# Five units of the first attention group scored between the qkv tiles, the attention output turned in the values' banks, and the second inverse root by Newton steps on VectorE

## What is computed

```python
x = x + attn(cond(x, cond_1024))             # cond: gated experts; attn: 16 heads of 16
x = x + ffn(cond2(x, cond_1024[:, None, :])) # cond2: a scan over the sequence; ffn: top-1 of 8 experts

# attn
qkv = x @ w_qkv.T                            # (B, N, 3, H, D), D = 16
q, k = rms_norm(q), rms_norm(k)              # t * rsqrt(mean(t * t) + eps)
attn = softmax((q @ k.T) * D ** -0.5)
y = attn @ v
Vn = v / max(norm(v), 1e-12)
y = y - sum(y * Vn) * Vn
out = y @ w_proj.T
```

## Time and profile before

| | |
|---|---|
| timed runs | 841.95, 844.62, 845.19 us |
| profiled execution, its own time | 842.52 us |
| its span in the trace | 840.8 us |
| TensorE busy | 779.9 us (93%) |
| ScalarE busy | 525.8 us (63%) |
| VectorE busy | 460.7 us (55%) |
| GpSimd busy | 248.3 us (30%) |
| first to last exponential of the attention | 329.12 to 582.80 us |

### The profile page before, as it was taken

The page is one execution under the profiler, slowest core; times in us unless marked ns, Lnnn a source line. Parts: engine busy times, 40 slices in busy tenths (PEclk is TensorE's granted clock), DMA queues, the critical chain, the costliest instruction groups (busy, mean ns, idle before and its releaser), DMA issues.

```text
span 840.8 us, 13450 instructions
## 1 busy us (share of the span) xinstructions
PE 779.9 (93%) x4456; PEld 511.6 (61%) x4456; DVE 460.7 (55%) x828; ACT 525.8 (63%) x699; POOL 248.3 (30%) x308
## 2 busy tenths in 40 slices
PE   8999999998999999889999989998789799999995
PEld 5778888886777875233222222223645588888884
DVE  3887666478766651533201202202447589999994
ACT  4432222463223236988999999997435288888883
POOL 5344444233433404200000000000000347777762
PEclk9999999999999999999999999999999899999999
DMA  9041111100234038064551342300178931111000
GB/s 251 18 77 51 50 49 43 34 26 26 101 113 135 4 43 107 1 115 162 76 76 27 49 75 36 39 0 0 51 266 283 337 126 49 52 51 53 25 11 0
DMA packets 52674, 64.87 MB, mean 77 GB/s; under 512 B 15889, under 2 KB 43929, under 8 KB 52636
## 3 DMA queue, kind: packets, MB, share of 16 engines
q1 hardware_dynamic: 44564, 55.96, 26.5%
q0 software_dynamic: 3312, 6.31, 2.5%
q10 hardware_dynamic: 4760, 2.12, 0.9%
HBM read 51.52 MB, written 15.60 MB: 80 GB/s over the span
## 4 chain that ended last, share of the span: by engine, by line
PE 67%; ACT 13%; DVE 9%; issue 8%; DMA 2%; ACTq 0%; SPq 0%; POOLq 0%; DVEq 0%
PE psum L1575 45%; ACT pexp L874 10%; PE psum L1727 7%; PE psum L1715 4%; PE psum L1931 2%; PE psum L1831 2%; DVE hl L1023 2%; DVE hh L1172 1%; PE psum L1845 1%; PE psum L1781 1%; DVE yT L1271 1%; PE psum L1678 1%; DMA x_tm<-in_x 1%; DVE ssum L1212 1%; DMA xs<-x_d,token_s 1%
## 5 line engine op out<-in xcount | busy, mean ns | idle before, releaser
L874 ACT ACTIVATE pexp<-psum 128x1024 f32<-128x1024 f32 x256 | 237.7, 1090 | 12.9 <-PE psum L1715 12.8
L801 ACT ACTIVATE hid<-psum,b_col 128x512 f32<-128x512 f32 x96 | 66.0, 688 | 160.5 <-PE psum L1575 107.2
L1727 PE MATMUL psum<-pexp,v_ones 128*32 128x512 f32 x1024 | 137.2, 609 | 18.5 <-ACT pexp L874 11.5
L1172 DVE TENSOR_SCALAR hh<-hid,scale_col 128x341 fp32r<-128x341 f32 x192 | 69.4, 403 | 70.5 <-ACT hid L801 53.6
L1715 PEld LDWEIGHTS psum<-q_stack,k_stack 48*128 48x128 f32 x512 | 39.2, 185 | 110.4 <-ACT pexp L874 92.8
L1715 PE MATMUL psum<-q_stack,k_stack 48*128 48x512 f32 x512 | 95.7, 449 | 7.2 <-DVE parts L1265 3.5
L1023 DVE SCALAR_TENSOR_TENSOR hl<-hid,scale_col,hh 128x341 fp32r<-128x341 f32 x192 | 96.3, 543 | 3.4
L1575 PE MATMUL psum<-hh,w2h 128*128 128x512 f32 x192 | 76.4, 398 | 4.0 <-DVE hl L1023 3.9
L1575 PE MATMUL psum<-x_hi,w1h 128*128 128x512 f32 x192 | 77.5, 404 | 0.1
L1575 PE MATMUL psum<-x_hi,w1l 128*128 128x512 f32 x192 | 75.6, 394 | 0.0
L1575 PE MATMUL psum<-x_lo,w1h 128*128 128x512 f32 x192 | 75.4, 393 | 0.0
(11 more groups left out here) (277 smaller groups left out, 1478.3 us busy)
## 6 DMA issues: line engine op xcount, KB each, us to landing
w_all<-in_L_ffn_W SPq DMA_DIRECT2D x16, 1024.0 KB, 12.9
raw<-in_L_cond_ew SPq DMA_DIRECT2D x32, 256.0 KB, 3.1
parts_d<-parts SPq DMA_DIRECT2D x8, 1024.0 KB, 5.0
q_stack<-parts_d SPq DMA_DIRECT2D x48, 128.0 KB, 4.7
k_stack<-parts_d SPq DMA_DIRECT2D x48, 128.0 KB, 7.4
raw<-in_L_cond_sw SPq DMA_DIRECT2D x16, 256.0 KB, 3.5
x_d<-x_tm SPq DMA_DIRECT2D x2, 1024.0 KB, 5.0
x_d<-x_tm ACTq DMA_DIRECT2D x4, 512.0 KB, 3.6
```

What stands on the lines that cost most here:

```text
L801: act.activation(hid[k % 4][:], bank(k % 4), ACT.Gelu_apprx_tanh, bias=b1_col[:, bass.ds(4 * q + k // 2, 1)]).then_inc(gelu_done, 1)
L874: act.activation(pexp[mt % 2][:, 2 * j:2 * j + 2, 512 * h:512 * h + 512], psum[:, 2 * r:2 * r + 2, :], ACT.Exp, scale=D ** -0.5)\
L1172: ins = dve.tensor_scalar(hh[k % 4][:, x0:x1], hid[k % 4][:, x0:x1], w[r], None, ALU.mult)
L1727: ins = pe.matmul(psum[VW * j:VW * j + VW, 6 + h, :], v_ones[i][:, mt, j, :], pexp[mt % 2][:, j, 512 * h:512 * h + 512], start=(mt == 0), ...
```

## The change

1. Scores of units 0 and 1 of group 0 are made behind qkv tile 4, unit 2 behind tile 5, unit 3 behind tile 6 and unit 4 behind tile 7 (`EARLY`), in banks 0 and 1 or 6 and 7; their exponentials stand between ScalarE's copies. The exponential of `decay` stands behind the copies of tile 0.
2. The ring starts with unit 5 and runs on over all groups. The output's turn goes to banks 6 and 7 behind unit 5 of the next group and takes no slot. Turns of q and k stand behind units 14 and 22 of groups 1 and 2. Blocks of values have a table: in groups 1 to 7 block 0 stands behind unit 8, and the next behind 9, 11, 12, 14, 15, 16, 18 and so on by twos; blocks 14 and 15 behind units 0 and 2 of the next group.
3. For batch 1, `root(1)` and the reciprocal are replaced by `inverse_root`: an integer first guess and three Newton steps, 14 instructions on VectorE over 256 elements per partition.
4. The groups are written out on TensorE and ScalarE instead of a loop; GpSimd's preparation of `v_ones` no longer waits for the qkv copies; SyncE's stores of the parts move to its steps for groups 2 and 3; the two matmuls of L1749 go.

```diff
+UNITS = HG * LT
+QK_AT = [(1, 14), (1, 22), (2, 14), (2, 22)]
+VALUES_AFTER = [8, 9, 11, 12, 14, 15] + [2 * v + 4 for v in range(6, LT + LT)]
+FIRST_VALUES_AFTER = [6, 7] + [2 * v + 4 for v in range(2, LT + LT)]
+EARLY = {4: (0, 1), 5: (2,), 6: (3,), 7: (4,)}
+EARLY_PAIR = (0, 3, 0, 3, 0)
+TURN_AFTER = 5
...
+        def pair(entry):
+            n = order.index(entry)
+            return EARLY_PAIR[n] if n < len(EARLY_PAIR) else (n - len(EARLY_PAIR) + 1) % 3
...
             sp.wait_ge(unit_done, 2 * FC * STEPS)
             for g in range(GROUPS):
                 load_stacks(g)
-                if g == 1:
-                    store_parts(1, 0)
-                if g == 2:
-                    for k in range(1, 4):
-                        store_parts(1, k)
+                if 2 <= g <= 3:
+                    for k in range(2):
+                        store_parts(1, 2 * g - 4 + k)
...
-            pool.wait_ge(qkv_out, TT)
+            pool.wait_ge(unit_done, 2 * FC * STEPS)
...
                 if g == 1:
+                    pool.wait_ge(qkv_out, TT)
...
+            def exp_unit(g, u):
+                mt, h, j = u // HG, u % HG // 2, u % 2
+                r = pair(("scores", g, u))
+                act.wait_ge(scored, UNITS * g + u + 1)
+                if u % 2 == 0:
+                    after(act, av_done, 2 * LT * g + u // 2 - 3)
+                act.activation(pexp[mt % 2][:, 2 * j:2 * j + 2, 512 * h:512 * h + 512],
+                               psum[:, 2 * r:2 * r + 2, :], ACT.Exp, scale=D ** -0.5)\
+                    .then_inc(exp_done, 1)
...
             def qkv_to_sbuf(b):
                 for i in range(LT):
                     act.wait_ge(qkv_made, b * LT + i + 1)
                     act.copy(qk_tm[b][:, i, :], bank(qkv_bank(i)))
                     act.copy(v_tm[:, b * LT + i, :], bank(qkv_bank(i) + 1)[:, 0:C]).then_inc(qkv_out, 1)
+                    if b and i == 0:
+                        decay_exp()
+                    elif b and i in EARLY:
+                        for u in EARLY[i]:
+                            exp_unit(0, u)
...
-                    if isinstance(g, int) and g == 0 and u == 19:
-                        root(1)
...
+            def inverse_root():
+
+                ms, r, t = ssum[:, :, 0:2 * H], inv_root[0], inv_root[1]
+                dve.wait_ge(var_made, 2)
+                nlink(dve.tensor_scalar(r[:].bitcast(I32), ms.bitcast(I32), 1, None, ALU.arith_shift_right))
+                nlink(dve.tensor_scalar(r[:].bitcast(I32), r[:].bitcast(I32), -1.0, float(0x5f3759df),
+                                        ALU.mult, ALU.add))
+                for _ in range(3):
+                    nlink(dve.tensor_tensor(t[:], r[:], r[:], ALU.mult))
+                    nlink(dve.tensor_tensor(t[:], t[:], ms, ALU.mult))
+                    nlink(dve.tensor_scalar(t[:], t[:], -0.5, 1.5, ALU.mult, ALU.add))
+                    nlink(dve.tensor_tensor(r[:], r[:], t[:], ALU.mult))
...
-            split_parts(0)
             take_output(0)
-            split_parts(1)
-            split_parts(2)
             finish_group(0, 0)
-            split_parts(3)
-            take_output(1)
-            finish_group(0, 1)
-            with dve.Fori(2, H // HG) as hg:
+            for hg in range(1, 3):
+                for k in range(2):
+                    split_parts(2 * hg - 2 + k)
+                take_output(hg)
+                finish_group(0, hg)
+            with dve.Fori(3, H // HG) as hg:
...
+            def turn(g):
+
+                pe.wait_ge(yT_out, g + 1)
+                for i in range(LT):
+                    ins = pe.transpose(psum[:, 6 + i // 4, (i % 4) * P:(i % 4 + 1) * P],
+                                       yT[:, i * P:(i + 1) * P], ident[:])
+                ins.then_inc(y_turned, 1)
...
+            def slot_free(n):
+
+                if n < 2:
+                    return
+                if len(EARLY_PAIR) <= n < len(EARLY_PAIR) + 2:
+                    pe.wait_ge(qkv_out, TT - len(EARLY_PAIR) - 1 + n)
+                    return
+                what, g, u = order[n - 2 if n < len(EARLY_PAIR) else n - 3]
+                if what == "scores":
+                    pe.wait_ge(exp_done, UNITS * g + u + 1)
+                else:
+                    pe.wait_ge(part_lo, 8 + g + 1)
...
+            def values(g, v):
+
+                i, mt, h = g % 2, v // 2, v % 2
+                pe.wait_ge(exp_done, UNITS * g + max(2 * v + 2, 4))
+                if v == 0:
+                    pe.wait_ge(v_ready, g + 1)
+                    after(pe, y_read, g)
...
+                    if b and i in EARLY:
+                        for u in EARLY[i]:
+                            if u == 0:
+                                pe.wait_ge(stack_in[0], 16 * 2 * LOADS)
+                                pe.wait_ge(y_split, 4 * NB)
+                            slot_free(u)
+                            scores(0, u, EARLY_PAIR[u])
```

More of the change, by code:

```diff
@@ L1634, in _, with fill_in @@
+            def fill_in(g, u):
+                at = VALUES_AFTER if g else FIRST_VALUES_AFTER
+                if g and u + UNITS in VALUES_AFTER:
+                    values(g - 1, VALUES_AFTER.index(u + UNITS))
+                if g and u == TURN_AFTER:
+                    turn(g - 1)
+                if u in at:
+                    values(g, at.index(u))
             for b in range(NB):
@@ L1704, in pair_free @@
+            for n, (what, g, u) in enumerate(order):
+                if n < len(EARLY_PAIR):
+                    continue
+                if what == "scores" and u == 0:
+                    pe.wait_ge(stack_in[g % 2], 16 * LOADS * (g - g % 2) + 16 * 2 * LOADS)
+                slot_free(n)
                 if what == "scores":
-                    pe.wait_ge(exp_done, PER * g + n + 1)
-                elif what == "turn":
-                    pe.wait_ge(y_read, g)
-                else:
-                    pe.wait_ge(part_lo, 8 + n + 1)
@@ L1757, in _ @@
-            pe.wait_ge(qkv_out, TT)
-            group(0, 0, first=True)
-            group(1, 1)
-            with pe.Fori(2, GROUPS, 2) as g:
-                group(g, 0)
-                group(g + 1, 1)
-            values(GROUPS - 1, 1, LT - 1, 0)
-            values(GROUPS - 1, 1, LT - 1, 1)
+                    scores(g, u, pair((what, g, u)))
+                    fill_in(g, u)
+                else:
+                    turn_b(g, pair((what, g, u)))
+            for v in range(2 * LT - 2, 2 * LT):
+                values(GROUPS - 1, v)
@@ L1799, in _ @@
                 if w == 0:
[L1800 removed]
+                    turn(GROUPS - 1)
             for w in range(4):
```

156 lines of the change are left out of this document (49 added, 107 removed).

## The result

| kernel | runs | median, us | ratio to the kernel before, 95% interval | first copy of batch 1 to end of the last exponential |
|---|---|---|---|---|
| before | 4 | 844.22 (841.95 to 845.19) | | 270.66 us |
| changed | 4 | 837.15 (837.0 to 838.41) | 0.9923, 0.9901 to 0.9946 | 265.51 us |
| changed, again, another chip session | 6 | 836.74 (835.9 to 839.71) | 0.9919, 0.9897 to 0.9941 | 264.66 us |

The forecast was 836.6 us. The profiled execution of the changed kernel took 837.02 us with a span of 835.3, 5.5 less than before. To see where they went I cut the span at marks that both traces have: the first copy of batch 1 (L811, now L832), the end of the last exponential, and the first exponential of the gates in the next stage.

What follows compares the result with a forecast made beforehand. ScalarE's exponentials bound the attention, but by little, so TensorE's order decides. Group 3 starts 5.9 us sooner, groups 3 to 7 give 0, the end -1.0: -7.0 from 843.6 gives 836.6 us, range 831 to 842.

Steps and rivals of the forecast that it cites:

- ScalarE's pace: Attention: exponentials in an unbroken row on ScalarE start 0.917 us apart, 29.3 us for a group of 32.
- The wait for the stacks: TensorE before qkv tile 5: stands still 3.15 us until the last load of group 0's stacks lands.
- Rival B: TensorE's clock falls after the wait before tile 5, costing 1.7 us; total 838.3 us; chance 0.20.
- Square root and tables: Group 0 on ScalarE: removing the square root and its table loads gives -3.1 us, and -0.5 for TensorE's clock.
- Group 0: 28 units at 0.917 us plus 0.3 for unit 9: group 1 starts at 358.5 instead of 363.03, -4.5 us.
- Turns of q and k: Groups 1 and 2: two turns in each; together 65.7 us against 67.1, about -1.4 us.
- Groups 3 to 7, nothing: Later groups: two removed gaps, 1.1 us per group, are offset by TensorE's catch-up with values, 1.16; length stays 30.5 us.
- Rival C: Catch-up in the groups isn't paid, since a single unit costs 0.33 us; -10.6, 833.0 us; chance 0.15.
- Normalization hidden: VectorE, batch 1: norms with the Newton operations end at 357.7, before group 0's output at 360.1; 3 us of room.
- Rival E: VectorE's Newton chain delays group 0's output; at 1.75 us per operation +15.7, in all 852.3 us; chance 0.05.
- The warming matmuls of L1749: Group 0: the two matmuls between the first scores go; they were hidden, so no time was set for them.
- End: Behind the last exponential: block 14 of values no longer waits for it, 0.95 us less; entered as -1.0.

Runs made afterwards that it cites:

- sqrt: Changed kernel with batch 1's square root back on ScalarE behind unit 19 of group 0 and the reciprocal back, no Newton steps; 841.67 us.
- turns: Changed kernel with only the turns of q and k moved, to units 12 and 28 of group 1 and 12 and 19 of group 2; 839.57 us.
- best: Changed kernel with the edits of late and turns and a values table without blocks behind single units in a row; 827.06 us.
- spread: Changed kernel with only the values table of groups 1 to 7 altered: blocks following a single unit lie behind units 9, 14, 19, 24; 835.23 us.
- Newton6: Changed kernel with six Newton steps instead of three, 12 more VectorE operations; 841.25 us.
- none: Changed kernel without early units: all 32 units of group 0 stand behind the qkv tiles; 837.23 us.
- tailwarm: Changed kernel with two unread matmuls put before TensorE's wait for `x_tm` behind the attention; 836.51 us.
- best2: best plus unread matmuls behind units 3 and 4 of group 0 and those of tailwarm behind the last exponential; 826.92 us.
- late: Changed kernel with two early units behind tile 6 and one behind tile 7, none behind tiles 4 and 5; 835.63 us.
- after2: The changed kernel itself, unedited, run again beside best and best2 on the same chip; 836.74 us.

## Why the forecast held, and where it didn't

- **ScalarE's pace** (0.917): misread; it is 0.903. So a group's floor is 28.9 us instead of 29.3, the square root's hole was 3.3 us instead of 3.1, and 28 exponentials take 0.4 us less than 25.7.
- **The wait for the stacks** (3.15): right in kind, 2.85 and 1.89 in two executions.
- **Rival B** (0.20) happened, close to its price, 1.5 of 1.7 us. I should have held it the likeliest: I set the rows of a fall after 2.57 us idle aside because the work around it was thin there. Dense tiles on both sides didn't help. The Trainium skill (TensorE: Matmul & The Clock Gate, Why this matters for your kernels) warns against idle gaps between bursts of matmuls. The traces agree at this place: seven waits of 1.89 to 3.08 us, seven falls.
- **Square root and tables** (-3.1 and -0.5): right in kind, a little small; sqrt gives 4.0 for both from the first scores on (3.5 from the first copy). The Trainium skill (ScalarE: Activation LUTs, What ACT_TABLE_LOAD costs) adds a drain of about the load's own length to each load; the rows of sqrt have the next instruction start 1.30 and 1.29 us behind the load's start, and the exponential ahead of the first load ends at 347.61, so no such drain is paid here.
- **Group 0**: group 1 was to start 46.4 us behind the first copy. It starts at 358.99, or 47.78: later by 1.4. Unit 4 is 1.65 late, nearly all of it B's fall; the pace gives 0.4 back, and unit 9's wait costs 0.1 more than said.
- **Turns of q and k** (65.7 us for groups 1 and 2): 65.65, where before had 66.89. The rules hold at other places too, as turns shows, and best for the two groups together.
- **Groups 3 to 7, nothing**: 152.08 us for the five instead of 152.88, so -0.8. Each loses 1.2 us at units 13, 16 and 17, as forecast; that the catch-up is the cause is shown by spread. Rival C needed a single unit of 0.33 us; TensorE's rows there say 0.42 (437.96 to 438.38).
- **Normalization hidden**: right. But its price beyond the room was sized by the wait alone. Newton6 cost 4.3 instead of 2.1, at least in part because TensorE stood still meanwhile and its clock fell. Rival E's 15.7 us lacked the same item, though that was not run.
- **The warming matmuls of L1749 "were hidden"**: hidden, but not idle in effect. The early units and early values took over their part; none shows what their place costs uncovered. I don't know from the runs what the kernel before would lose without them.
- **End** (-1.0): this step failed in the profile, +0.6. The block of values was saved (ctx's first copy starts 1.79 us after the last exponential instead of 2.66). `x_tm` comes from VectorE, which had not become as much faster: the next turn starts 15.22 us after the last exponential instead of 16.00, with 2.99 us of waiting in front instead of 2.64. Behind that the clock's falls took 1.4 back. What the forecast put at nothing is the clock: in all eleven profiles with these same instructions (all but before, tailwarm and best2) it falls 14 to 17 us behind the last exponential, and they reach the gates in 40.9 to 44.3 us, 42.9 on the average, which is also the one profile of before. With a single fall, 34 to 36 us behind the last exponential, stand before (42.93), tailwarm (42.09) and best2 (42.08), so at like clock the kernel is 0.85 us faster here, about what the block should give. The block's price is right; what is left of it in the time isn't measured.

So the total is right partly by luck. In the profiled execution B and the pace left 1.4 us of -7.0 missing in group 0, the end 1.6, groups 1 and 2 0.2; the later groups gave 0.8 more, and the first stage, outside the change, was 0.9 faster: -7.0 + 1.4 + 1.6 + 0.2 - 0.8 - 0.9 = -5.5, which is what was measured. The medians say -7.1 and -6.3, and the distance to the mean that the forecast was set against (843.6) is 6.5 and 6.9.

## What to carry to other kernels

When one engine is nearly saturated and another follows it closely, write down the few rules of the trace (cost of each piece alone and in a row, how late it may be) and run the order by them before moving anything. Take an engine's pace from single starts, not from the length of a merged row. The rules here gave the stretch to within 0.5 us for three orders of groups 1 to 7 that had not run (spread, turns, best), and the order found with them gained more than the change did. Where the clock fell in group 0 (none, late) the expectations missed the stretch by 2.4 and 1.3 us, since the rules had no term for it. Ask of every wait that you add or move on TensorE what it does to the clock behind it, and put independent matmuls into the wait, or move the waiting piece behind work that doesn't need it.

## What I had not expected of the hardware

- The length of the idle time doesn't tell whether the clock falls. It fell after 1.89 us in after2 and stayed up after 2.64 us in the kernel before; in none it fell with no idle time over 0.53 us since the last tile, among single units of scores with 0.41 between them.
- From the last exponential to the end the kernels run nearly the same instructions (only tailwarm and best2 add two), yet the 14 profiled executions (before, the changed kernel twice and the eleven others) took 257.3 to 260.3 us there. Where the clock falls in that part differs from one execution to the next (the changed kernel: 592 to 596 and 609 to 616 us; turns: 593 to 596 and 634 to 637), so a saving of 1 us there can't be told from one profile.
- Exponentials that follow each other start 0.903 us apart while their records mostly grow, from 1.02 to 1.18 us in a row of 22; so 0.24 us of waiting, as in front of unit 8 of the changed kernel's group 4, shows in no idle time.
- The last load of group 0's stacks is not landed at a fixed time: in the seven profiles with the plain wait, the scores that it releases start 10.3 to 11.5 us behind the first copy, with the same loads in the same order.
